# A recurrent block on one core: where a batch's closing gate, sum, turn and copy stand in the program

## What is computed

```
A:  h  = layernorm(x)                       # a normalised copy feeds both parts
    ys = selective_scan(h, forward) + selective_scan(h, backward)   # 16 states each way
    x1 = x + ys * silu(ffn(h))              # the ffn is a router times a gelu MLP
B:  q  = rope(layernorm(x1) @ W_in.T)       # state-space block
    z, xBC, dt = split(rmsnorm(q) @ W_zxbcdt.T)
    xBC = silu(conv4(xBC))                  # 512 channels, 4 taps
    sm = rmsnorm(ssd(xBC, dt) * silu(z)) @ W_out.T + q
    yB = two layers of local attention and gelu MLP, on layernorm(x1)
    out = x1 + sm * silu(yB)                # the gate and the sum of this document
```

## Time and profile before

| | us |
|---|---|
| median of 3 runs | 4046.13 (4043.56 to 4046.46) |
| the profiled execution | 4043.23, its span 4041.4 |
| TensorE busy | 3221.6 (80%) |
| VectorE busy | 2563.5 (63%) |
| ScalarE busy | 2596.5 (64%) |
| GpSimd busy | 1725.4 (43%) |
| mean granted TensorE clock | 0.919 |

### The profile page before, as it was taken

How to read it: one execution, slowest core, us unless ns; L and a number is a source line. 1 busy time by engine, 2 the same in 40 slices (tenths; PEclk the granted TensorE clock), 3 DMA queues, 4 the chain that set the end, 5 groups by cost and what they waited for, 6 DMA issues and landing times.

```text
span 4041.4 us, 57661 instructions
## 1 busy us (share of the span) xinstructions
PE 3221.6 (80%) x17248; PEld 1887.2 (47%) x17248; DVE 2563.5 (63%) x4240; ACT 2596.5 (64%) x5871; POOL 1725.4 (43%) x1428
## 2 busy tenths in 40 slices
PE   4688888887888878787887888878888787878787
PEld 2254444544544445444544445445454454445453
DVE  5575676657667675666757666576576756666443
ACT  4466667665676756667666676656767666676555
POOL 2253353534435354344533535344353543545332
PEclk9799899998999989999999999989999899999999
DMA  2000000000000000000000000000000000000000
GB/s 85 3 1 1 6 1 6 1 1 6 1 7 1 1 7 1 7 1 2 6 1 6 1 7 1 1 6 1 7 1 1 7 1 7 1 1 4 1 3 3
DMA packets 18388, 20.58 MB, mean 5 GB/s; under 512 B 768, under 2 KB 17152, under 8 KB 17792
## 3 DMA queue, kind: packets, MB, share of 16 engines
q1 hardware_dynamic: 18048, 16.44, 1.2%
HBM read 12.24 MB, written 4.19 MB: 4 GB/s over the span
## 4 chain that ended last, share of the span: by engine, by line
PE 42%; DVE 17%; ACT 14%; POOL 13%; issue 12%; DMA 0%; POOLq 0%; DVEq 0%; ACTq 0%; SPq 0%
PE bank L568 9%; PE bank L630 6%; POOL hc L1479 4%; PE bank L822 3%; DVE hst L1250 3%; ACT Pm L1068 3%; PE bank L806 3%; POOL oT L1545 3%; POOL oT L1537 3%; POOL Pm L1552 2%; DVE tmp L1390 2%; PE bank L780 2%; PE bank L762 2%; PE bank L551 2%; DVE bank L1242 2%
## 5 line engine op out<-in xcount | busy, mean ns | idle before, releaser
L1479 POOL TENSOR_TENSOR hc<-hst,Cs 128x512 f32<-128x512 f32 x512 | 654.7, 1279 | 959.6 <-DVE hst L1250 946.9
L1250 DVE TENSOR_TENSOR_SCAN hst<-dA,bank 128x512 f32<-128x512 f32 x512 | 625.0, 1221 | 135.5 <-issue 58.8
L568 PE MATMUL bank<-W,xs 128*128 128x512 f32 x960 | 529.0, 688 | 139.0 <-DVE tmp L1390 135.6
L1242 DVE TENSOR_TENSOR bank<-u,bank 128x512 f32<-128x512 f32 x512 | 351.3, 686 | 163.0 <-PE bank L551 157.1
L936 ACT COPY Cs<-bank 128x512 f32<-128x512 f32 x512 | 298.6, 583 | 233.2 <-PE bank L551 204.1
L1552 POOL TENSOR_TENSOR Pm<-Pm,rinv 128x512 f32<-128x512 f32 x256 | 271.0, 1059 | 408.6 <-DVE rinv L1410 392.4
L551 PE MATMUL bank<-parts,sel 96*128 96x512 bf16 x1024 | 348.8, 415 | 109.1 <-DVE hst L1250 42.1
L1537 POOL TENSOR_TENSOR oT<-tmp 128x512 f32<-128x512 f32 x256 | 325.3, 1271 | 252.7 <-DVE tmp L1390 231.5
L930 ACT ACTIVATE dA<-delta,neg_a 128x512 f32<-128x512 f32 x512 | 372.4, 727 | 67.6 <-DVE hst L1250 66.9
L1068 ACT ACTIVATE Pm<-bank,mx 128x128 f32<-128x128 f32 x1024 | 365.2, 387 | 14.9 <-DVE mx L1404 14.8
L536 PE MATMUL bank<-C,hc 128*128 128x128 f32 x2048 | 341.9, 294 | 36.5 <-POOL hc L1479 36.4
(11 more groups left out here) (227 smaller groups left out, 6045.3 us busy)
## 6 DMA issues: line engine op xcount, KB each, us to landing
W<-wpack SPq DMA_DIRECT2D x1, 4498.0 KB, 13.2
x_tok<-x SPq DMA_DIRECT2D x16, 256.0 KB, 2.9
out<-xa SPq DMA_DIRECT2D x16, 256.0 KB, 2.3
rot<-tables SPq DMA_DIRECT2D x2, 512.0 KB, 15.9
wc_f<-taps SPq DMA_DIRECT2D x1, 1024.0 KB, 19.2
C<-cpack SPq DMA_DIRECT2D x1, 721.0 KB, 14.5
Pm<-mask SPq DMA_DIRECT2D x1, 320.0 KB, 14.8
tmp<-rowpack SPq DMA_DIRECT2D x1, 256.0 KB, 17.1
```

Source lines behind the costliest of these rows:

```text
L568: mm(b[:, :], weights, rhs, start=True, stop=True).then_inc(full(ring, job), 1)
L1242: v.tensor_tensor(b[:, :], u[:, d, :], b[:, :], ALU.mult).then_inc(sem("a_bx"), 1)
L1250: v.tensor_tensor_scan(o, a, b, 0.0, ALU.mult, ALU.add).then_inc(sem("a_h"), 1)
L1479: g_.tensor_tensor(hc[:, k % 2, :], hst[:, k % 2, :], Cs[:, k % 2, :], ALU.mult)\
```

## The change

Nothing is computed differently; instructions move. ScalarE's silu of the gate goes from the end of the batch's stage B (slot 51) into the next batch's stage B at slot 5, between the silus of cx0 and cx1. VectorE's product and sum go with it, to a new slot 5 behind four scan steps. TensorE's turn goes from slot 2 (ahead of cx0) to behind cx3 and ahead of mz0. ScalarE's copy to xo goes behind the silu of cx3, and the store follows it. The copy of x1 into x1b has to come after that and goes to slot 8. The two table loads around the gate's silu have no place any more, but for one at the very end.

```diff
@@ TensorE, stage_b @@
                 for t in range(4):
                     yield 2 + t
-                    if t == 0 and ended is not None:
-                        finish(ended)
                     if used("B", f"cx{t}", i):
...
                     last.then_inc(full("B", f"cx{t}"), 1)
+                if ended is not None:
+                    finish(ended)
                 for t in range(2):
                     norm_sum("B", f"mz{t}", i, wz_f[:, t * P:(t + 1) * P], hpad[:, 3:3 + T])
@@ ScalarE, stage_b @@
-                yield 2
-                if ended is not None:
-                    finish(ended)
-                act.wait_ge(*step("a_x1", i))
-                nc.scalar.copy(x1b[:, :], x1[:, :]).then_inc(sem("m_x1b"), 1)
                 for t in range(4):
                     yield 5
+                    if t == 1 and ended is not None:
+                        gate_out(ended)
                     act.wait_ge(*filled("B", f"cx{t}", i))
                     b = bank("B", f"cx{t}")
                     f(xbc[:, t, :], b[:, :], ACT.Silu, bias=w("convb", t, t + 1)).then_inc(sem("m_xs"), 1)
+                if ended is not None:
+                    copy_out(ended)
...
                 yield 8
                 shifted(xs0, xn2, "t_xs", "m_xn", i, 1)
+                act.wait_ge(*step("a_x1", i))
+                nc.scalar.copy(x1b[:, :], x1[:, :]).then_inc(sem("m_x1b"), 1)
...
-                yield B_END
+
+            def gate_out(i):
                 act.wait_ge(*step("f_y", i))
                 f(tmp2[:, 0, :], yB[:, :], ACT.Silu).then_inc(sem("g2"), 1)
-                tables()
-
-            def finish(i):
+
+            def copy_out(i):
                 act.wait_ge(*step("xo_full", i))
...
+            def finish(i):
+                gate_out(i)
+                copy_out(i)
@@ VectorE, stage_b @@
                     last.then_inc(sem("m_ld"), 1)
+                yield 5
+                if ended is not None:
+                    finish(ended)
                 yield 6
...
-                yield B_END
+
+            def finish(i):
                 dve.wait_ge(*step("g2", i))
                 v.tensor_tensor(tmp1[:, 0, :], sm[:, :], tmp2[:, 0, :], ALU.mult).then_inc(sem("x2a"), 1)
                 dve.wait_ge(*step("x2a", i))
                 v.tensor_tensor(x2[:, :], x1b[:, :], tmp1[:, 0, :], ALU.add).then_inc(sem("x2"), 1)
-
-            def finish(i):
-                pass
```

## The result

| | before | changed |
|---|---|---|
| median | 4045.73 (4043.56 to 4046.46, 4 runs) | 4013.09 (4006.11 to 4025.28, 4 runs) |
| ratio, with its 95% interval | | 0.9924 (0.9906 to 0.9943) |
| the profiled execution, its span | 4043.23, 4041.4 | 4013.81, 4012.0 |
| mean granted TensorE clock | 0.919 | 0.923 |

The forecast was 4014.3 us, and 4011.4 for a profiled execution. In the profile's page of the changed kernel (busy us, share, instructions) ScalarE has 31 instructions fewer than in the earlier trace rows; they are table loads. VectorE has as many as before.

What follows compares the result with a forecast made beforehand. No engine is full; VectorE is late in stage B's tail and delays TensorE's restart. 4043.2 - 31.8 + 0 = 4011.4 us profiled, 4014.3 against the median (chance 0.70), range 4000 to 4034.

Steps and rivals of the forecast that it cites:

- Part 1: End of stage B: removing VectorE's two gate instructions saves 2.27 us in each of 14 tails, 31.8 us.
- rival (c): No gain: the branch paces the restart or another engine fills the 2.27 us; 4046 us within 8; chance 0.07.
- Part 2: Same tail: the 3.24 us of table loads and silu leaving ScalarE are the same time, no further gain.
- rival (b): More gain: clock stays at 2.4 GHz after the restart (3974 us), or ScalarE holds the tail (4001); chance 0.07.
- Part 3: New place in the next stage B: moved work fits idle time, with 1.6 us slack before the turn; cost 0.
- The bound of 4 us: New place: most it could cost in all if GpSimd's hc slowed both VectorE gate instructions by 0.95 us each.
- The sum: Whole kernel: 4043.2 - 31.8 + 0 = 4011.4 us for a profiled execution, 4014.3 against the median.
- rival (a): Clock takes back 16 us after the restart, or 20 us through slow fourth convolutions; 4026 to 4035 us; chance 0.13.
- Rival (d): Slower: low clock reaches past the restart, the first convolution takes 3.44 us more per tail; 4062 us; chance 0.03.

Runs made afterwards that it cites:

- e3: The changed kernel plus two additional VectorE instructions, SBUF operands only, at the gate's old place in the tail; 4041.21 us, ratio 1.0001 to the kernel before.
- e1: The changed kernel, but ScalarE's silu of the gate and its two table loads stay at the end of stage B; 4027.09 us, ratio 0.9968.
- g1: The changed kernel plus four additional VectorE products (2.87 us) ahead of the gate's product at the new place; 4033.49 us, ratio 0.9985.
- e2: The kernel before with only the turn, the copy to xo and the copy of x1 moved to their new places; 4039.72 us, ratio 0.9996.
- h1: The changed kernel measured again, unaltered; 4020.80 us, ratio 0.9929 to the kernel before.
- f2: The changed kernel plus small additional TensorE matmuls ahead of the tail's last three scan steps; 4026.77 us, ratio 0.9961.
- f3: The changed kernel plus additional TensorE matmuls both in the tail's last scan steps and in the pause ahead of the fourth convolution; 4027.45 us, ratio 0.9968.
- e4: The changed kernel plus two additional VectorE instructions in the tail, one operand of each in PSUM; 4049.04 us, ratio 1.0019.
- f1: The changed kernel plus two additional TensorE matmuls in the pause ahead of the fourth convolution; 4000.70 us, ratio 0.9898.
- h2: The kernel before plus two additional TensorE matmuls in the pause ahead of the fourth convolution; 4039.93 us, ratio 0.9986.
- h3: The changed kernel plus two additional matmuls ahead of the fourth convolution and two ahead of the norm's sum; 3997.33 us, ratio 0.9875.

## Why the prediction was right

*Part 1, VectorE's 2.27 us per tail.* Right, in place, size and count: forecast 31.8 us, measured 30.8. The pitch of 1.85 is unbroken, and e3 returns the tail's gain with two VectorE instructions and nothing else. TensorE's pause before the restart grew by 0.09 us in the mean, 1.0 us over the eleven tails with a branch, and not by what VectorE saved: rival (c) falls, and this is the 1.0 us that is missing.

*Part 2, ScalarE's 3.24 us are the same time.* Right. With its work put back, e1 loses 0.9 of 30.8 us in the tail, and the form of rival (b) in which ScalarE holds the tail falls. 31 loads of 1.283 us, 39.8 us, left ScalarE (its busy time on the page fell by 38.3), and VectorE passed on 0.9 us of that.

*Part 3, what the next step pays.* The silu second in its row, the sum of 0.69 us, the idle VectorE, the 1.6 us of slack, the turn at 0.43 us in both places and the hidden copies: all as read, in the rows after, in g1 and in e2. mz's first silu starts 0.86 us before the second, which is the time of mz's two matmuls in between, so it starts when its bank is filled. The bound of 4 us from a meeting with GpSimd was not reached: hc ends 0.05 us before the product starts. The margin is thin, and a meeting was not tried at the new place; in e3, in the tail, both engines were seen to lose. The prediction says that the bound would be reached if hc ended later than the silu. That is too much: in e3 the sum ends 0.55 us behind hc, so an hc that is late by a little would delay the product by about that little.

*The sum.* 4011.4 forecast for the profiled execution, 4013.8 measured. That this is within 3 us is partly luck: two terms that the sum does not have nearly cancel. One step failed, the count in rival (a): the slow fourth convolution was put as "seen in 2 of 14 steps" and as something that spreads to the twelve others or does not. It was 4 of 15 before, and it spread to four of the eleven others, so 6.6 us of the gain went there, and 5.9 us came from the other side, in the stretch behind the restart. Terms of some 7 us from the clock, one each way, belonged into the sum. Both look like effects of the shorter tail and not of one execution: the four profiles with the short tail and no filling (changed, h1, e1, g1) show 8, 8, 8 and 9 slow convolutions and 80.0, 78.9, 82.7 and 82.2 us from first block to first convolution. With the turn moved but the tail as long as before it is 3 and 84.2 us (e2), and none and 85.5 us (e3). Why the shorter tail does either was not found. Rival (d) also doubles the time of a convolution at low clock, where the slow ones here take 1.70 us more, not 3.44, with the clock at 0.65 in the mean. Rival (a) in its first form, the rise of the clock fixed in time, did not happen: the windows behind the restart show a low clock no longer than in the earlier trace rows.

```profile
2144.88:2148.80 3.92, 1.11 (x5) 0.71 (x4) 2.25 (x3) 1.31 (x2) 2.52 (x2) 0.50 0.04 10
2148.80:2153.40 4.60, 4.57 (x24) 4.19 (x25) 2.85 (x6) 0.58 (x1) 1.26 (x1) 0.60 0.02 5
```

It is 0.60 in the mean over the first 4.60 us, where the earlier trace rows have 0.50 over 4.80. Rival (b) in its larger form, no low clock behind the restart, did not come either, and f2 shows that even a dense tail does not bring it in the loop. Rival (d) falls by the same windows.

## What to carry to other kernels

The price of an instruction in an unbroken chain is the distance from it to the next one in the timeline, a delay by its neighbour included. The busy time that leaves an engine which was early (here 39.8 us of table loads) is no gain. Then look for a place where every engine concerned is idle or already set up, and compare two starts, that of the reader and the end of the moved work. If TensorE waits some 2 us between dense stretches, look at each instance of the matmul behind the wait for two durations (3.70 and 5.40 here), and try to fill the wait with matmuls that need nothing: here two such matmuls brought the ratio from 0.9924 to 0.9898, at 1.72 us in the one step that had no wait to fill. More filling is not more gain: f3, with the tail filled too, was at 0.9968.

## What was not expected of the hardware

- A pause of 2.23 us at 2.4 GHz is followed by 1.2 GHz in some steps (8 of 15 in the changed kernel, 4 before, none in e3 and e4) and not in others. A pause of 0.52 us never was (none of 15 in each of f1, f3, h2 and h3).
- The pause of the loop's branch, 3.0 to 3.5 us in f2, is followed by 1.2 GHz even when TensorE was at 2.4 GHz until it began.
- Executions of one program lie up to 12 us from their median, and in two profiles of the changed kernel the difference is in stretches that hang on the clock. Edits shift the clock in stretches that they do not touch as well, beyond that scatter (e1 lies 0.004 above the changed kernel's ratio, e4 0.005 above its forecast, both outside the intervals). So a total is not evidence for a mechanism of that size; the stretch in which it works is.
- A VectorE sum of two SBUF tiles beside a GpSimd product takes 1.63 us instead of 0.69, and the product 1.62 instead of 1.27. With one operand in PSUM the sum takes 0.69.
